# Cross-attention plus spline FFN on one core: the loop over batches unrolled, attention products moved between the gate tiles, energies taken two batches ahead

## The reference, cut to what matters

```python
# per batch; everything float32
q, k   = ctx @ Wq.T + bq, ctx @ Wk.T + bk          # ctx 512x256, q and k 512x128
att    = softmax(q @ k.T)                          # 512x512
x      = x + layernorm(x) @ att.T                  # (b, l, n) x (b, m, n) -> (b, l, m)
gate_w, up_w, down_w = spline(gate_cp), spline(up_cp), spline(down_cp)   # 2048x512, 2048x512, 512x2048
h      = layernorm(x)
x      = x + (silu(h @ gate_w.T) * (h @ up_w.T)) @ down_w.T
```

## Time and profile before

| | us |
|---|---|
| three runs, median | 311.19 |
| profiled execution: whole time | 310.87 |
| its span on the core | 308.7 |
| busy: PE, DVE, POOL, ACT | 254.3, 202.2, 154.3, 138.5 |
| mean granted TensorE clock | 0.912 of full speed |

### The profile page before, as it was taken

One profiled execution on the slowest core, in us unless ns is written; L12 is line 12 of the kernel. 1 busy time (PEld: TensorE's weight loads), 2 busy tenths in 40 slices (PEclk: granted clock), 3 DMA queues, 4 the chain that ended last, 5 costly groups with the idle time before them and its releaser, 6 DMA issues.

```text
span 308.7 us, 4074 instructions
## 1 busy us (share of the span) xinstructions
PE 254.3 (82%) x1320; PEld 158.4 (51%) x1320; DVE 202.2 (65%) x348; ACT 138.5 (45%) x229; POOL 154.3 (50%) x158
## 2 busy tenths in 40 slices
PE   5979519868797889998867999979679999576995
PEld 1323107632333646786334568863436689253484
DVE  1665795674759886575598765756988557478523
ACT  3043414310736586225758642267589131745420
POOL 0987930263675559321463692304829722077810
PEclk9775857995969799999999899999999999959999
DMA  6799600000007000001280000013500000300003
GB/s 221 289 271 381 264 0 0 1 1 2 0 13 328 0 3 0 2 0 68 74 333 0 0 0 0 0 70 95 243 0 0 0 0 14 122 0 2 0 2 136
DMA packets 6938, 22.65 MB, mean 73 GB/s; under 512 B 1168, under 2 KB 2320, under 8 KB 5456
## 3 DMA queue, kind: packets, MB, share of 16 engines
q1 hardware_dynamic: 6928, 22.52, 20.1%
HBM read 18.32 MB, written 4.19 MB: 73 GB/s over the span
## 4 chain that ended last, share of the span: by engine, by line
PE 36%; issue 25%; POOL 22%; DVE 10%; ACT 4%; DMA 1%; SPq 1%; POOLq 0%; DVEq 0%; ACTq 0%
POOL ih L1188 10%; PE bank L1348 5%; POOL xl L1120 4%; PE bank L1350 4%; PE bank L1349 4%; PE bank L1440 4%; POOL xres L1175 3%; PE bank L1222 3%; PE bank L1400 3%; PE bank L1235 2%; POOL gw L1102 2%; PE bank L1325 2%; PE bank L1248 2%; PE bank L1447 1%; PE bank L1414 1%
## 5 line engine op out<-in xcount | busy, mean ns | idle before, releaser
L1188 POOL TENSOR_TENSOR ih<-inter,ones 128x512 fp32r<-128x512 f32 x64 | 64.5, 1040 | 38.4 <-DVE inter L1018 38.4
L1400 PE MATMUL bank<-mv,gw 128*128 128x512 f32 x128 | 47.5, 469 | 17.8 <-DVE inter L1018 9.2
L1018 DVE TENSOR_TENSOR inter<-inter,bank 128x512 f32<-128x512 f32 x64 | 42.1, 682 | 6.6 <-ACT inter L828 5.1
L828 ACT ACTIVATE inter<-bank 128x512 f32<-128x512 f32 x64 | 37.0, 597 | 20.1 <-PE bank L1400 18.6
L1400 PEld LDWEIGHTS bank<-mv,gw 128*128 128x128 f32 x128 | 23.7, 202 | 40.8 <-DVE inter L1018 18.0
L1440 PEld LDWEIGHTS bank<-d_r,ih 128*128 128x128 f32 x256 | 35.3, 188 | 7.9 <-issue 5.0
L1440 PE MATMUL bank<-d_r,ih 128*128 128x288 f32 x256 | 38.2, 299 | 0.0
L799 ACT ACTIVATE qk<-bank,nmr,rstd 128x512 f32<-128x512 f32 x16 | 12.5, 780 | 43.2 <-PE bank L1350 26.9
L1159 POOL TENSOR_TENSOR ve<-mv,eps 128x1 f32<-128x1 f32 x16 | 5.6, 347 | 47.5 <-DVE mv L989 47.5
L1175 POOL TENSOR_TENSOR xres<-x,ones 128x2048 f32<-128x2048 f32 x4 | 14.4, 3600 | 28.8 <-DMA out<-xres 28.5
L1348 PE MATMUL bank<-ph,xh 128*128 128x512 f32 x64 | 25.5, 399 | 2.1 <-POOL xl L1120 2.1
(11 more groups left out here) (98 smaller groups left out, 434.0 us busy)
## 6 DMA issues: line engine op xcount, KB each, us to landing
x<-in_x SPq DMA_DIRECT2D x4, 1024.0 KB, 4.9
xT<-in_xT SPq DMA_DIRECT2D x4, 1024.0 KB, 7.2
out<-xres SPq DMA_DIRECT2D x16, 256.0 KB, 2.0
rd<-in_d_r SPq DMA_DIRECT2D x1, 2304.0 KB, 22.4
ctxT<-in_ctxT SPq DMA_DIRECT2D x4, 512.0 KB, 7.1
d_coef<-in_d_coef SPq DMA_DIRECT2D x1, 1024.0 KB, 15.8
d_pt<-in_d_node SPq DMA_DIRECT2D x1, 1024.0 KB, 17.4
knots<-in_d_knot SPq DMA_DIRECT2D x1, 640.0 KB, 13.2
```

The source lines that it names most:

```text
L828: nc.scalar.activation(inter[:, m], gbank[m % 2][:], ACT.Silu).then_inc(s["silu_done"], 1)
L1018: V.tensor_tensor(inter[:, m], inter[:, m], ubank[m % 2][:], ALU.mult).then_inc(s["mult_done"], 1)
L1188: G.tensor_tensor(ih[:, m], inter[:, m], ones[:, 0].broadcast_to([P, TOK]), ALU.mult).then_inc(s["ih_done"], 1)
L1400: mm(dst[m % 2][:], gw[:, n, m // 2, m % 2 * P:(m % 2 + 1) * P], mv[:, m // 2], start=True, stop=True).then_inc(s[done], 1)
```

## The change

The loop over batches becomes straight code, and there are three lists: `attention_first`, then `gates(b)` and `downs(b)` for each b. With a = b + 1 and c = b + 2:

- `attention_first` does the spline weights, the whole attention of batch 0 up to its `project` and `functions`, and q, k, energies, softmax and first statistics of batch 1. `keep_warm` is left at one place with 6 matmuls. q and k of batch 0 come before the first spline corrections. Half of each correction of `gw` moves from POOL to DVE (`upper`).
- `gates(b)` does the 16 gate tiles of b, and between them the transposed attention, the attention product and most of the residual and second layernorm of a. The product is split over the tiles: `xm(a, n, p)` does 6 matmuls. `inter` holds 8 tiles in place of 16. Every fourth tile (in the last batch every second) is rounded on ACT.
- `downs(b)` does the down product of b, between its parts q, k, energies, softmax and first statistics of c, and the transpose, `project` and `functions` of a.
- The four `replicate` stages become two `functions` stages: two matmuls each, a high part by ACT, a low part by DVE into `zs`, and then SP issues 24 DMAs of 20 rows that copy the parts to their places in `mv` (`place`).
- For b > 0 the scaling of the attention moves from DVE to POOL (`scale`). `split_x` is done in two halves.
- The buffer x is one of three (`x0`, `x1`, `x2`, batch 3 uses `x0` again); the copy to `xres` and the wait in front of it are gone, the output is added into x and stored from there.
- Some buffers share space: `xn2T` with `ph`, `xn2` with `zs`, the low parts of q and k with `pl`.

```diff
+        def gates(st, b):
+            a = b + 1
+            more = a < B
+            if more:
+                for t in range(2):
+                    st.prob_t(a, t)
...
+            gate(0)
+            gate(1)
+            if more:
+                st.prob_t(a, 2)
+            gate(2)
+            if more:
+                st.xm(a, 0, 0)
+                st.prob_t(a, 3)
+            gate(3)
+            if more:
+                st.xm(a, 1, 0)
...
+            gate(7)
+            if more:
+                st.xm(a, 3, 0)
+                for t in range(2):
+                    st.scale_xm(a, t)
+            gate(8)
+            if more:
+                st.add_xm(a, 0)
+                st.xm(a, 0, 1)
+            gate(9)
+            if more:
+                st.normalise(a, 0)
+                st.add_xm(a, 1)
+                st.xm(a, 1, 1)
...
+        def downs(st, b):
+            a, c = b + 1, b + 2
+            if c < B:
+                st.qk(c, 0)
+            if a < B:
+                st.normalise(a, 3)
+            st.down_basis(b, 3)
+            if c < B:
+                st.qk(c, 1)
+            st.half_split(b)
+            if c < B:
+                st.exp_table()
+            st.down(b, 0)
+            if a < B:
+                for t in range(2):
+                    st.norm_t(a, t)
+                    st.cast_t(a, t)
+            st.gather_halves(b)
+            if a < B:
+                for t in range(2, NT):
+                    st.norm_t(a, t)
+                    st.cast_t(a, t)
+            st.down_split(b)
+            st.down(b, 1)
+            if a < B:
+                st.project(a)
+            for t in range(2):
+                st.down_tail(b, t)
+                st.add_out(b, t)
+            if c < B:
+                for t in range(2):
+                    st.energy(c, t)
+                    st.softmax(c, t)
+            if a < B:
+                for j in range(2):
+                    st.functions(a, j)
+            st.down(b, 2)
+            if c < B:
+                for t in range(2, NT):
+                    st.energy(c, t)
+                    st.softmax(c, t)
+                st.scale(c)
+                for h in range(2):
+                    st.split_x(c, h)
+            st.down_tail(b, 2)
+            st.add_out(b, 2)
+            st.down(b, 3)
+            if c < B:
+                st.stats(c)
+                st.mean_shift(c)
+                st.silu_table(c)
+            st.down_tail(b, 3)
+            st.add_out(b, 3)
...
             # POOL
                 def scale(b):
+                    if b:
+                        pool.wait_ge(s["rinv_done"], b + 1)
+                        for t in range(NT):
+                            G.tensor_tensor(prob[:, t], prob[:, t], rinv[:, t].broadcast_to([P, TOK]), ALU.mult)
...
+                def split_x(b, h):
+                    pool.wait_ge(s["xh_done"], 2 * b + h + 1)
+                    part = slice(2 * h, 2 * h + 2)
+                    G.tensor_tensor(xl[:, part], xT[:, part], xh[:, part].bitcast(f32), ALU.subtract)
...
             # DVE, unchanged: the first layernorm's shift waits for POOL's rstd1 of that batch
                 def mean_shift(b):
                     dve.wait_ge(s["rstd1_done"], b + 1)
...
             # PE: the first gate tiles wait for the sums of the batch before
+                        elif b:
+                            pe.wait_ge(s["out_added"], NT * (b - 1) + 2 * n + m + 1)
...
             # SP
+            def place(b, j):
+                sp.wait_ge(s["zs_done"], 2 * b + j + 1)
+                for i in range(CLS):
+                    a = CLS * j + i
+                    base = 0 if a % 2 else HALF
+                    for k, z in enumerate((0, 1, 0)):
+                        rows_to = slice(base + k * G_FN, base + (k + 1) * G_FN)
+                        sp.dma_start(mv[rows_to, a].bitcast(f32), zs[QUAD * i:QUAD * i + G_FN, 2 * j + z].bitcast(f32))
...
             # the end of attention_first
+            for t in range(NT):
+                st.energy(1, t)
+                st.softmax(1, t)
+            st.scale(1)
+            st.stats(1)
+            st.mean_shift(1)
+            st.silu_table(0)
```

More of the change, by code:

```diff
@@ L528, in attention_only @@
+            st.project(0)
+            for n in range(2):
+                st.qk(1, n)
+            for j in range(2):
+                st.functions(0, j)
+            for h in range(2):
+                st.split_x(1, h)
             for r in range(20, 24):
                 st.spread(r)
-        def ffn(st, b, a=None):
-            st.project(b)
-            if a is not None:
-                st.qk(a, 0)
-            for t in range(2):
-                st.replicate(b, t)
-            if a is not None:
-                st.qk(a, 1)
-            for m in range(4):
+                st.residual(r)
@@ L607, in ffn @@
-            st.gather_halves(b)
-            if a is not None:
-                for t in range(1, 3):
-                    st.xm(a, t)
-                st.mean_shift(a)
-                st.add_xm(a, 0)
-            st.down_split(b)
-            if a is not None:
-                for t in range(1, 4):
-                    st.add_xm(a, t)
-                st.xm(a, 3)
-            st.down(b, 2, range(0, 16))
+                if m and on_scalar(b, m - 1):
+                    st.round_inter(b, m - 1)
@@ new lines, in gates @@
+            gate(7)
[8 more added lines that the diff above has]
+            gate(9)
+            if more:
+                st.normalise(a, 0)
+                st.add_xm(a, 1)
+                st.xm(a, 1, 1)
+            gate(10)
+            st.down_basis(b, 1)
+            gate(11)
+            if more:
+                st.normalise(a, 1)
+                st.xm(a, 2, 1)
@@ L693, in _ @@
-            sp.wait_ge(s["qk_mm"], 2)
-            sp.dma_start(ctxT[:], d["ctxT"][1]).then_inc(s["ctx_in"], 16)
-            with sp.Fori(0, B - 2) as b:
-                batch(b, True)
-            batch(B - 2, False)
-            for t in range(NT):
-                store(B - 1, t)
-            sp.wait_ge(s["out_stored"], 16 * NT * B + 1)
+                sp.dma_start(out[b, t], x[b][:, t]).then_inc(s["out_stored"], 16)
+            columns(1)
+            sp.wait_ge(s["consts_set"], 1)
+            for j in range(2):
+                place(0, j)
@@ L702, in _ @@
+            for b in range(B):
+                if b + 2 < B:
+                    rows(b + 2)
+                    context(b + 2)
+                    columns(b + 2)
+                for t in range(2):
+                    store(b, t)
+                if b + 1 < B:
+                    for j in range(2):
+                        place(b + 1, j)
+                for t in range(2, NT):
+                    store(b, t)
+            sp.wait_ge(s["out_stored"], 16 * NT * B)
         @block.scalar
@@ L864, in constants, with keep_warm @@
                     V.memset(eps[:], EPS)
[L865 to L868 removed]
+                    V.memset(ones[:], 1.0)
+                    V.memset(neghalf[:], -0.5)
+                    for a in range(G_CLS):
+                        rows = slice(QUAD, HALF) if a % 2 else slice(HALF + QUAD, P)
+                        last = V.memset(mv[rows, a].bitcast(f32), 0.0)
+                    last.then_inc(s["consts_set"], 1)
+                def keep_warm(n, dst):
                     pass
```

800 lines of the change are left out of this document (396 added, 404 removed).

## The result

| | kernel before | changed kernel |
|---|---|---|
| median of runs, us | 310.81 (309.16 to 312.0, 4 runs) | 330.11 (328.78 to 331.28, 4 runs) |
| profiled execution, whole / span | 310.87 / 308.7 | 329.91 / 328.1 |
| mean granted TensorE clock | 0.912 | 0.842 |

The changed kernel is slower: ratio 1.0624, 95% interval 1.0559 to 1.0689. The sign is as predicted, but the loss is 19.3 us where 6.7 was forecast. The time lies at the upper end of the stated range, 298 to 331, which reaches there only for the sake of rival 2; the forecast's own was 312 to 323.

What follows compares the result with a forecast made beforehand. It took the kernel to be bound by waits, no engine holding the chain. 114 + 60 + 60 + 49 + 32 = 315 us of span, with 2.2 around it 317, taken as 317.5; range 298 to 331, the forecast's own 312 to 323.

Steps and rivals of the forecast that it cites:

- rival 2: DVE and POOL shut each other out in the gates' second half and the prologue: 335 us with all, 327 half; chance 0.18.
- The sign: Whole kernel: slower than before by more than 0.5%, chance 0.59; faster 0.32, same 0.09.
- The reason in one line: Pipeline one stage deeper: filling costs 20.5 us more, third batch gives back 10, last 3.5, turns stay at 60.
- on which I rest most: End of `downs`: DVE's `mean_shift` waits for POOL's scalings, split and `rstd1` until 35 us, 8.5 us of PE's path.
- 8 us or more: Batches 2 and 3: DVE idle that long before `mean_shift` or the first sum after it, released by POOL.
- 3 us late without it: Turns: placement DMAs end at 29.3 us, hidden behind POOL's chain, late by this much if that chain were gone.
- the placement's issue: SyncE's queue after the functions' low part: twelve DMAs take 5.6 us to issue plus 2.0 to land.
- the third batch: Gates 25 us and downs 24, 49 in all; no table load, energies or `mean_shift`, functions landing at 24.
- wherever PE has just waited: Stretch before the first gates: PE's matmuls after a wait priced at the lower clock, 1.2 GHz.
- Last batch: Gates 15 us with the start, then basis, halves, down product, output and store 17: 32 against 35.6.
- The prologue: Stretch before the first gates: 114 us where it was 93.5, bounds 101 and 119.
- Rival 1: Shorter or earlier POOL chain lets the turn fall to about 55 us, prologue 107: 298 us; chance 0.31.

Runs made afterwards that it cites:

- Number 1: Changed kernel with `mean_shift` of batches 2 and 3 moved from `downs` into the gates of the batch before: 323.96 us, 6.1 below the changed kernel.
- number 2: Changed kernel with 8 of each 24 placement DMAs left, so values differ: 323.49 us, 6.6 below the changed kernel.
- 3: Changed kernel with one semaphore per class, so a gate tile waits for its class's three copies, not all twelve: 325.68 us, 4.4 below the changed kernel.
- 5: Changed kernel with the last batch's placements of every second class issued from ScalarE's queue: 328.71 us, not to be told from the changed kernel.
- 10: Changed kernel with late statistics and `mean_shift`, semaphores per class, late node sums, scaling on DVE, and POOL's split of batches 2 and 3 waiting for it: 305.34 us.
- 6: Changed kernel with POOL's four node products put just behind the first knot sums in the prologue: 326.17 us, 3.9 below the changed kernel.
- 7: Changed kernel with `down_nodes` (DVE's sums of node products, ACT's copy) moved behind the split of x of batch 1: 323.17 us, 6.9 below the changed kernel.
- 8: Kernel before with 6 of its 60 filler matmuls: 310.82 us, ratio 1.01, no difference that can be told.
- 9: Changed kernel with late first-layernorm statistics and `mean_shift`, one semaphore per class, late node sums, and scaling back on DVE: 315.3 us, 14.8 below the changed kernel.

## Why the prediction was right, and where it failed

**What held.** The reason in one line held: the filling costs some 22 us, and the turns, which should pay for it, stay at 60. The step "on which I rest most" held: DVE waits at `mean_shift`, released by POOL behind scalings, split and `rstd1` (the run of POOL is 166.20 to 176.1). Counted from PE's last gate matmul (its end, 141.06, in the first turn), PE's work ends at 26.8 us (26.5 predicted) and POOL's at 35.05 (35). The mark of "8 us or more" was not met, 6.58 measured: DVE fills the first 3.4 us of the stretch with an output sum and four statistics. Number 1 shows that the wait is on the path. Its price there is 6.1 us for two turns. By the prediction it would be 5.5 a turn, 8.5 less the "3 us late without it" of the placement; the slower placements, which release the first gate at 173.42, 2.7 us before `mean_shift`, and POOL's scaling ahead of them took the rest.

**What failed: the placement's issue, a term of the sum.** The end was to give back 10 us in the third batch and 3.5 in the last; by the same cuts it gave back 2.3 and 0.9. "With a little between the issues twelve DMAs take 5.6 + 2": an SP issue of a load had 0.43, and I took this for a copy within SBUF. Such a copy of 20 rows took 0.706, 0.75 apart, so twelve take 9.0 us: +3.4. I bounded the landing, which was right, from both sides, and the issue not at all. The turns hold the same error: in the first, SP begins 21.7 us behind the last gate, as predicted, and the gates are released at 32.4, not 29.3. There it costs nothing, since POOL covers it (number 2); in `downs(2)`, where by the prediction itself the functions land last (at 24, PE done at 21.3), it stands open. Numbers 2, 3 and 5 show it from three sides: fewer copies, finer waits, two queues. Number 2 puts what hangs on their late end at 7.7 us.

**The same stage, second part.** The first low part of the functions, which releases the first twelve copies, ended 20.1 us after the third batch's last gate and not 16.4, which makes the other 3.7 (less 0.4 of a shorter landing). PE stood 3.34 us for DVE's last product, as predicted (3.3). Then basis and the first down product ran from 266.20 to 272.30 at a mean granted clock of 0.50, that is at the lower level of 1.2 GHz, and took 6.1 us where the earlier trace rows at 2.4 GHz give 3.2. I had counted the wait and taken the lower clock in the prologue "wherever PE has just waited", but not here. The same wait stands in numbers 1 and 10 (3.35 and 3.36), and there the same work took 4.94 us at a mean granted clock of 0.65. So with the wait alike it is the clock that sets the price; no run takes the wait itself away.

**Last batch, +2.7.** Its gates took 16.8 us in place of 15, the rest 17.9 in place of 17. The gates' share is the placements' again: 0.66 is the ninth gate's wait for the second twelve, and the others started at the lower clock behind the wait of 5.94. In number 2, without these waits, the gates take the 15.0 predicted. For the rest I have no run.

**The prologue, +1.4.** It has the waits named: PE idle 10.41 us before the second half of the product ("ten us"), released through `d_coef` (changed kernel, PE and DVE; the `qk` copy on ACT stands behind DVE's sums):

```profile
61.98 0.80 PE L1442 MATMUL bank<-ph,xh 128*128 128x512 f32 x1 [10.41 <-ACT qk L849]
...
58.65 1.23 DVE L1023 TENSOR_TENSOR d_coef<-d_coef 128x1024 f32<-128x1024 f32 x1 [5.87 <-POOL d_coef L1215]
```

Numbers 6 and 7 took 3.9 and 6.9 us from that stage alone, so it was a wait and not work. Number 8 shows no effect of the fillers in the kernel before.

**The rivals.** Rival 1 needed a shorter chain on POOL. With that chain taken apart (number 10) the turn is 54.9 to 57.6 us, its "about 55": the pipeline can pay, by 1.4%. The prologue there, 103.5, is shorter than rival 1's 107, but by number 7's move and not by the clock that rival 1 named. Rival 2, the lock, put the time at 327 to 335 (with all its terms the upper end adds up to 340), and the measured 330 lies there by luck. The lock cost little in the changed kernel: `normalise` has a median of 1.08 us where it had 0.52, 16 of them, up to 9 us of DVE, but most of it in time that DVE had; the third batch's gates came out 0.8 us over, where rival 2 needs 2.5 to 6 a batch. Where it was decisive is the place that I did not look at, the scaling against the split. There number 9 and 10 differ by one wait and by 10.0 us. What the traces show is that a `TENSOR_SCALAR` with one SBUF input is held by a subtraction on POOL: four scalings in 5.91 us beside it, in 1.68 without. The Trainium skill ("SBUF — State Buffer", section "Who interferes with whom") says of this form that it can run in a mode with two ports and then contends with GpSimd for the pair that they share, whichever issues first holding it for the whole instruction. The traces agree: two scalings were done before the split, and each of the other two ended behind one of its two instructions. I had read that section for its two-input rule alone, for which `add_xm` would have been the danger; in the changed kernel its sum kept 0.68 us, and a rounding beside it (130.77) took 1.42 where others take 1.04. In number 7, beside the node products, two of the sums took 0.85 and 1.66.

## What to carry to other kernels

A deeper pipeline pays only if the turn gets shorter: list, engine by engine, what each turn's first instruction waits for, since the second and third wait stand just behind the first. Price a small DMA by its own kind: the issue sits on one queue and repeats, and what the steady state hides stands open in the last turn. Keep GpSimd's large elementwise work away from the VectorE instructions on which TensorE waits; a wait added on GpSimd can be worth more than the work that it delays.

## What the runs showed of the hardware that was not expected

- The same matmuls behind the same wait of PE (3.34 to 3.36 us) took 6.10 us at a mean granted clock of 0.50 in the changed kernel and 4.94 at 0.65 in numbers 1 and 10.
- An issue of an SBUF to SBUF copy of 20 rows costs SP 0.706 us (16 rows: median 0.589), where a load's took 0.43 at the start of the kernel; ScalarE's queue needs 0.727 for the same and issues at the same time.
- A `TENSOR_SCALAR` of 128x512 on DVE takes 0.48 us by itself. Two of them that met POOL's two subtractions (2.36 and 2.52 us) took 2.63 and 2.56, each ending 0.3 us behind one of these.
